# Attention scores for the row maxima, computed as pairs of heads on row groups of the matmul array

## The reference, cut to what matters

```python
    # B, T, D, H = 2, 1024, 128, 16 ; HD = 8
    q, k, v = (proj(Wq, bq), proj(Wk, bk), proj(Wv, bv))
    q = q * cos + rotate_half(q) * sin
    k = k * cos + rotate_half(k) * sin
    attn = jnp.einsum('bhqd,bhkd->bhqk', q, k) * scale
    attn = jax.nn.softmax(attn, axis=-1)
    out = jnp.einsum('bhqk,bhkd->bhqd', attn, v)
```

## Time and profile before

| | before |
|---|---|
| median of 3 runs | 1059.84 us (1059.75 to 1062.03) |
| profiled execution, its own time | 1058.78 us |
| span of its trace, first to last instruction | 1057.0 us |
| mean granted PE clock | 0.906 |
| PE busy | 862.0 us (82%) |
| DVE busy | 862.0 us (82%) |
| ACT busy | 572.5 us (54%) |
| attention passes, on PE | from 88.57 us |

### The profile page before, as it was taken

The page is one execution under the profiler, slowest core; times in us unless marked ns, Lnnn a source line. Parts: engine busy times, 40 slices in busy tenths (PEclk is TensorE's granted clock), DMA queues, the critical chain, the costliest instruction groups (busy, mean ns, idle before and its releaser), DMA issues. The chain is left out here.

```text
span 1057.0 us, 12554 instructions
## 1 busy us (share of the span) xinstructions
PE 862.0 (82%) x3703; PEld 392.3 (37%) x3703; DVE 862.0 (82%) x795; ACT 572.5 (54%) x897; POOL 238.8 (23%) x131
## 2 busy tenths in 40 slices
PE   5589999989999949985464457777777579999998
PEld 2212222222222212224342222222222266888886
DVE  6698888878888748828956899999999873888886
ACT  2304777767777737882131642332333165888885
POOL 3700000000000000100110156776777620123110
PEclk9857999999999979998677788998999867999999
DMA  7440020110101030003000233444444002122111
GB/s 174 128 132 1 11 56 24 54 58 12 56 11 57 14 99 11 11 20 85 0 1 0 89 119 118 160 158 140 158 159 158 21 1 83 60 97 83 60 60 41
DMA packets 37977, 73.51 MB, mean 70 GB/s; under 512 B 7299, under 2 KB 21627, under 8 KB 36891
## 3 DMA queue, kind: packets, MB, share of 16 engines
q1 hardware_dynamic: 37922, 72.82, 21.7%
HBM read 62.50 MB, written 8.85 MB: 68 GB/s over the span
## 5 line engine op out<-in xcount | busy, mean ns | idle before, releaser
L970 DVE TENSOR_REDUCE nmax<-ps 128x1 f32<-128x1024 f32 x256 | 301.0, 1218 | 57.3 <-PE ps L1291 57.3
L738 ACT ACTIVATE prob<-ps 128x512 f32<-128x512 f32 x512 | 265.7, 605 | 137.1 <-PE ps L1310 136.8
L1291 PE MATMUL ps<-ks,qs 96*128 96x512 bf16 x512 | 206.3, 416 | 29.7 <-DVE nmax L970 18.1
L1310 PE MATMUL ps<-qs,ks 96*128 96x512 bf16 x512 | 194.7, 389 | 7.0 <-ACT prob L738 3.3
L670 POOL TENSOR_TENSOR hc<-hst,cbr 128x1024 f32<-128x1024 f32 x64 | 153.4, 2398 | 93.1 <-DVE hst L1107 93.1
L1489 PE MATMUL ps<-hc,ident 128*128 128x512 f32 x256 | 134.4, 650 | 41.7 <-POOL hc L670 38.8
L862 ACT ACTIVATE ps<-dt,a_neg 128x1024 f32<-128x1024 f32 x64 | 71.5, 1118 | 145.9 <-DVE hst L1107 145.9
L1107 DVE TENSOR_TENSOR_SCAN hst<-ps,dbx 128x1024 f32<-128x1024 f32 x64 | 145.6, 2276 | 0.0
L1327 PE MATMUL ps<-prob,vq 128*16 128x512 f32 x1024 | 133.6, 598 | 0.8 <-ACT prob L738 0.7
L1174 DVE TENSOR_TENSOR act_l<-act_t,act_h 128x1024 fp32r<-128x1024 f32 x64 | 92.1, 1449 | 35.5 <-ACT act_h L903 35.5
L1310 PEld LDWEIGHTS ps<-qs,ks 96*128 96x128 bf16 x512 | 49.6, 98 | 164.6 <-ACT prob L738 117.5
(11 more groups left out here) (176 smaller groups left out, 969.7 us busy)
## 6 DMA issues: line engine op xcount, KB each, us to landing
cbr<-s_dram SPq DMA_DIRECT2D x64, 512.0 KB, 3.6
gate<-c_dram SPq DMA_DIRECT2D x8, 1024.0 KB, 6.7
qs<-q_dram SPq DMA_DIRECT2D x18, 288.0 KB
ks<-k_dram SPq DMA_DIRECT2D x54, 96.0 KB
o_dram<-o_sb SPq DMA_DIRECT2D x16, 256.0 KB, 2.1
wf<-in_L_ffn_w SPq DMA_DIRECT2D x8, 256.0 KB, 2.8
wfq<-in_L_ffn_w SPq DMA_DIRECT2D x8, 256.0 KB, 3.1
q_dram<-parts SPq DMA_DIRECT2D x16, 96.0 KB, 2.1
```

Source lines behind the costliest of these rows:

```text
L738: nc.scalar.activation(prob[:, n % 8], ps[:, 4 + (first + n) % 3], ACT.Exp, scale=ATT_SCALE).then_inc(s_exp, 1)
L970: nc.vector.tensor_reduce(nmax[:, half, n:n + 1], ps[:, 2 * (t % 2):2 * (t % 2) + 2, :], AX.XY, ALU.max, negate=True).then_inc(s_max, 1)
L1291: mm = nc.tensor.matmul(ps[:, 2 * (t % 2) + kk], qs[p][:, half, h, q * P:(q + 1) * P], ks[p][:, kk, h, :], start=True, stop=True)
L1310: nc.tensor.matmul(ps[:, 4 + (first + n) % 3], ks[p][:, kt // 4, j, kt % 4 * P:(kt % 4 + 1) * P], qs[p][:, half, j, :], start=True, stop=T ...
```

## The change

- The untransposed score tiles, whose only use is the maxima, are made by `score_pair` in place of `score_half`. They use two bf16 parts of q and k in place of three: 4 products of 8 numbers, 32 rows for each head. The four heads lie in four row groups of new tiles `qm[p]` and `km[p]`; one pair is two heads, 128 queries by 512 keys each.
- DVE's reduce gives one maximum for each head (two outputs for 1024 inputs); one `tensor_tensor` with `min` per half pass joins the two halves of the keys.
- The new tiles are filled by `load_heads`: 2 x 4 x 3 = 24 DMAs for each set, issued on the SP queue immediately before `load`, at the start for three sets and then in each of passes 0 to 5.
- In a step both pairs come in one place, after the fourth matmul of line 1310 and before `products`.
- `rden` becomes a view of the tile `sq`.

```diff
+        qm, km = ([sb(f"{w}{n}", [P, 2, BANK], BF16) for n in range(SETS)] for w in ("qm", "km"))
...
+        nmax_k = sb("nmax_k", [P, 2, 2, QUAD, 4])
...
-        rden = sb("rden", [P, BATCH, SEQ])
+        rden = sq[:].rearrange("p (b t) c -> p b (t c)", b=BATCH)
...
+            def load_heads(it, p):
+
+                for f in range(2):
+                    for h in range(QUAD):
+                        q, k = (t[bass.ds(it, 1), f].rearrange("o n (d h) t -> (o n d) h t", h=QUAD)[0:2 * HD, h]
+                                for t in (q_dram, k_dram))
+                        sp.dma_start(km[p][32 * h:32 * h + 32, f], k.unsqueeze(0).to_broadcast([2, 2 * HD, BANK])).then_inc(s_qm[p], 16)
+                        for a in range(2):
+                            sp.dma_start(qm[p][32 * h + 16 * a:32 * h + 16 * a + 16, f],
+                                         q[HD * a:HD * a + HD].unsqueeze(0).to_broadcast([2, HD, BANK])).then_inc(s_qm[p], 16)
...
             for p in range(SETS):
+                load_heads(p, p)
                 load(p, p)
...
                 if again is not None:
                     sp.wait_ge(s_pv, STEPS * (it + 1))
+                    load_heads(again, p)
                     load(again, p)
...
-                        dve.wait_ge(s_score, 32 * it + t + 1)
-                        nc.vector.tensor_reduce(nmax[:, half, n:n + 1], ps[:, 2 * (t % 2):2 * (t % 2) + 2, :],
-                                                AX.XY, ALU.max, negate=True).then_inc(s_max, 1)
...
+                        u = 16 * half + n
+                        qt, kk, pair = n // 4, n % 4 // 2, n % 2
+                        dve.wait_ge(s_score, 32 * it + u + 1)
+                        nc.vector.tensor_reduce(nmax_k[:, half, kk, 2 * pair:2 * pair + 2, qt], ps[:, 2 * pair:2 * pair + 2, :],
+                                                AX.X, ALU.max, negate=True).then_inc(s_max, 1)
+                    w = 3 * (2 * it + half)
                     dve.wait_ge(s_max, 32 * it + 16 * half + 16)
+                    nc.vector.tensor_tensor(nmax[:, half], nmax_k[:, half, 0].rearrange("p h q -> p (h q)"),
+                                            nmax_k[:, half, 1].rearrange("p h q -> p (h q)"), ALU.min).then_inc(s_mstep, 1)
...
+            def score_pair(it, p, u):
+
+                half, qt, kk, pair = u // 16, u % 16 // 4, u % 4 // 2, u % 2
+                if not (isinstance(it, int) and it == 0 and u < 2):
+                    pe.wait_ge(s_max, 32 * it + u - 1)
+                for n in range(2):
+                    rows = slice(32 * (2 * pair + n), 32 * (2 * pair + n + 1))
+                    mm = nc.tensor.matmul(ps[:, 2 * pair + n], qm[p][rows, half, qt * P:(qt + 1) * P],
+                                          km[p][rows, kk, :], start=True, stop=True)
+                mm.then_inc(s_score, 1)
...
-                        for t, kk in todo[len(todo) * j // 4:len(todo) * (j + 1) // 4]:
-                            score_half(it + 1, (p + 1) % SETS, t, kk)
+                        if more and j == QUAD - 1:
+                            for u in range(MAX_TILES):
+                                score_pair(it + 1, (p + 1) % SETS, MAX_TILES * s + u)
                         if s >= 1 and j == (QUAD - 1 if more else QUAD - 2):
                             products(it, p, s - 1)
```

More of the change, by code:

```diff
@@ L227, in build_kernel @@
         s_qk = [sem(f"s_qk{n}") for n in range(SETS)]
+        s_qm = [sem(f"s_qm{n}") for n in range(SETS)]
         s_score = sem("s_score")
@@ L439, in build_kernel @@
         LOADS = 16 * (2 * (PARTS + 1) + 1)
+        HEAD_LOADS = 16 * 2 * 3 * QUAD
         @block.sync
@@ L967, in maxima @@
                     for n in range(16):
-                        t = 16 * half + n
-                        dve.wait_ge(s_score, 32 * it + t + 1)
-                        nc.vector.tensor_reduce(nmax[:, half, n:n + 1], ps[:, 2 * (t % 2):2 * (t % 2) + 2, :],
-                                                AX.XY, ALU.max, negate=True).then_inc(s_max, 1)
-                    w = 2 * (2 * it + half)
+                        u = 16 * half + n
[4 more added lines that the diff above has]
+                    w = 3 * (2 * it + half)
                     dve.wait_ge(s_max, 32 * it + 16 * half + 16)
+                    nc.vector.tensor_tensor(nmax[:, half], nmax_k[:, half, 0].rearrange("p h q -> p (h q)"),
+                                            nmax_k[:, half, 1].rearrange("p h q -> p (h q)"), ALU.min).then_inc(s_mstep, 1)
+                    dve.wait_ge(s_mstep, w + 1)
                     nc.vector.tensor_copy(nmax_p[:, 0:16], nmax[:, half]).then_inc(s_mstep, 1)
-                    dve.wait_ge(s_mstep, w + 1)
+                    dve.wait_ge(s_mstep, w + 2)
                     nc.vector.tensor_tensor(nmax_p[:, 16:32], nmax[:, half], nmax_p[:, 0:16], ALU.subtract).then_inc(s_mstep, 1)
-                    dve.wait_ge(s_mstep, w + 2)
+                    dve.wait_ge(s_mstep, w + 3)
                     dve.wait_ge(s_nrow[half], 64 * it)
@@ L1008, in _ @@
             dve.wait_ge(s_qk[SETS - 1], LOADS * (PASSES // SETS + 1))
+            dve.wait_ge(s_qm[SETS - 1], HEAD_LOADS * (PASSES // SETS + 1))
             quant(0, wf[:], wfq[:], (s_wf, 16 * 5), scaled=lambda: norm_dve_var(1, 0), before_last=lambda: norm_dve_scale(1, 0))
@@ L1284, in _, with one_pass @@
                 mm.then_inc(s_v_ps, 1)
[L1286 to L1296, removed]
+            def score_pair(it, p, u):
[7 more added lines that the diff above has]
+                mm.then_inc(s_score, 1)
+            def one_pass(it, p, first, loads, more, between={}):
+                pe.wait_ge(s_qk[p], LOADS * loads)
                 for s in range(STEPS):
@@ L1303, in one_pass @@
                     if more and s == 0:
-                        pe.wait_ge(s_qk[(p + 1) % SETS], LOADS * loads)
-                    todo = [(MAX_TILES * s + n // 2, n % 2) for n in range(2 * MAX_TILES)] if more else []
+                        pe.wait_ge(s_qm[(p + 1) % SETS], HEAD_LOADS * (loads + (p + 1) // SETS))
                     for j in range(QUAD):
@@ L1329, in products @@
                 mm.then_inc(s_pv, 1)
-            pe.wait_ge(s_qk[0], LOADS)
+            pe.wait_ge(s_qm[0], HEAD_LOADS)
             pe.wait_ge(s_v, 4)
-            for t in range(32):
-                score_half(0, 0, t, 0)
-                score_half(0, 0, t, 1)
+            for u in range(32):
+                score_pair(0, 0, u)
             with pe.Fori(0, PASSES // SETS) as r:
                 for p in range(SETS):
-                    one_pass(SETS * r + p, p, 4 * STEPS * p, True, r + 1 + (p + 1) // SETS)
-            one_pass(PASSES - 2, 0, 0, True, PASSES // SETS + 1)
+                    one_pass(SETS * r + p, p, 4 * STEPS * p, r + 1, True)
+            one_pass(PASSES - 2, 0, 0, PASSES // SETS + 1, True)
             def project_out(b):
@@ L1412, in turn_first_x @@
                 turn_x(1, 1)
-            one_pass(PASSES - 1, 1, 4 * STEPS, False, between={1: lambda: project_out(0), 8: turn_weights, 12: turn_first_x})
+            one_pass(PASSES - 1, 1, 4 * STEPS, PASSES // SETS + 1, False, between={1: lambda: project_out(0), 8: turn_weights, 12: turn_first_x})
             pe.wait_ge(s_wft, 3)
```

## The result

The changed kernel takes 1164.14 us (median of 4 runs, 1159.64 to 1166.09) against 1060.28 us before: the ratio is 1.097, 95% interval 1.0936 to 1.1005. The forecast was 1168 us. The profiled execution took 1166.09 us, its span is 1164.3 us.

The account below looks back on a forecast made before the run. The passes were taken to run at PE's pace, with SP's added DMAs delaying it: 44.8 + 8.5 + 18.3 + 35.7 + 1 = 108.3 us on 1058.8 gives 1167.1, forecast 1168 us, range 1137 to 1199.

Parts of the forecast that it names:

- Start: Before pass 0: 72 added DMA issues at 0.70 us delay the first maxima; pass 0 starts 35.7 us later.
- Passes 1, 2, 4, 5: PE stalls 9.4 us at step 8 for second-half maxima, plus 1.8 us of lowered clock: 44.8 us in all.
- Pass 3: Same step 8 stall, less because PE already starts 2.7 us late: 6.7 + 1.8 = 8.5 us.
- pass 6: `den` comes 18.3 us later behind SP's issues, delaying DVE's maxima of pass 7 and PE's second step: 18.3 us.
- Steps: 72 steps outside the waits take 2.83 us, row-group savings lost to waiting for ACT: about 1 us in all.
- P: Time of a step's pair matmuls on PE: 0.22 us if all overlap, 0.87 if none; about 0.34 taken.
- Rival 1: SP's added issues are cheap, 0.436 us each, so stalls total about 57 us: 1117 us; chance 0.15.
- rival 2: Row groups on PE don't overlap: step 3.36 us, 40 us more, 1206 us; chance 0.14.
- Rival 3: The added DMAs' transfers are slow, carried by few engines, 4.7 us more at nine places: about 1210 us; chance 0.06.
- Rival 4: Kernel gets faster: step falls to DVE's 2.35 us and SP's work hides, ending near 1055 us; chance 0.05.
- The range: Total time from 1137 us at 0.60 us an SP issue to 1199 at 0.90, the latter adding about 139 us.

Follow-up runs that it names:

- the run with two queues: Changed kernel with heads issued earlier, in mid pass, start reordered, pairs before the fourth matmul, and ACT issuing all `km` DMAs before pass 0: 1059.95 us, ratio 0.9998.
- the best version: Changed kernel with earlier mid-pass heads, reordered start, pairs before the fourth matmul, rows over more DMA engines, ACT issuing sets 1 and 2's heads at start: 1051.91 us.

## Why the prediction was right

The time and the cause were right, and the terms can be laid against the account above. That the sum came out within 1 us of the trace (108.3 forecast, 107.3 measured) is luck in part: single terms are off by 1 to 3 us both ways, and 4.5 us of what was measured, in pass 0 and from pass 7 on, had no term of its own.

- **Start, 35.7 us forecast, 32.6 measured.** The last stores of parts ended 46.5 us later, not 50.4: an issue with its gap took 0.65 us, not 0.70. The price came from line 503, whose shape is like theirs but whose issue is longer: 0.684 us against 0.624. SP then waited 1.6 us before the maxima, for which the forecast had nothing, and PE started 1.3 us after the fourth of them was issued, not 2.1. What followed had no term: the granted clock was 0.51 from 121 to 133 us, and pass 0 took 1.4 us more than before.
- **Passes 1, 2, 4, 5, 44.8 us forecast, 43.1 measured.** Step 8 resumed 31.1 us after the pass began; the forecast had 31.5. Two errors in it nearly cancel: the 24 issues took 18.9 us, not 18.3, and PE started 1.3 us after the fourth issue's end and not 2.1. The 2.1 us were read from stores of 256 KB, and those of the maxima have 2 KB. That the clock falls after a stall of 8.65 us, as it did after 13.70, was needed for this term and held (0.50 from 201 to 207 us).
- **Pass 3, 8.5 us forecast, 7.3 measured; pass 6, 18.3 forecast, 19.8 measured.** That the same queue delay would come out in full through `den` was read from a stall that PE already had. PE's wait grew by 17.8 us. The other 2 us are the clock behind the stall, at half for some 7 us in place of 4 (0.50 from 485 to 494 us, with PE at work from 487.15; before, 0.50 from 383 to 387).
- **Steps, 2.83 us forecast, 2.71 and 2.83 in turn.** Both values were in the forecast, as bounds of P: 2.71 when all four run together, 2.83 when DVE holds the second pair. I took one as the rule where they alternate. In 72 steps that is 4 us. The wait of the fourth matmul for the first exponential was forecast 1.08 us after the first and stands there. It takes back 0.43 of the 0.65 us that the four matmuls save.
- **Rival 1** (cheap issues) falls by the 0.62 us, **rival 2** (row groups don't overlap) by the 0.32 us from the pairs to the products. The Trainium skill (TensorE: Matmul & The Clock Gate, Measured speedup vs the span model) gave an estimated 0.28 us for the four. In the trace the 0.32 us hold the change to the products too, some 0.1 us, which leaves 0.22: the four ran wholly together, and faster than that estimate. The mean step, 2.77 us, equals the one that the estimate gave, but by chance: it is the mean of 2.71 and DVE's 2.83.
- **Rival 3** (slow transfers) was wrong for the changed kernel and right as a mechanism. In the run with two queues an average of 1.8 engines carried them, and a set took some 17.8 us from the first issue (40.92) to the first pair (58.72), though its issues took only 11.3 us; with another dimension outermost it took 5 us less. The Trainium skill (DMA: Bandwidth & Descriptors, Why a DMA increments its semaphore by 16 and not by 1) gives these DMAs two engines, and the trace agrees with 1.8.
- **Rival 4** (faster): the part of it that lies on PE is real. With the issues out of the way and the pairs in front of the fourth matmul, the best version is 7 us below the kernel before. The kernel before with SP's and ACT's work at the start in the new order was not run; in its trace PE never waits for a DMA of the maxima, so little of the 7 us should be due to the order alone, but this is argued. Three things remain in the way. DVE's buffer of two makes every other step long. The start is later: 53.97 us for the first pair in the best version, against 50.76 for the first such matmul before. And the clock falls more often: passes 4 and 5 of the best version take 44.6 us at a granted clock of 0.96, where its pass 1 takes 43.0 at 1.00; the kernel before has 1.00 in both.
- **The range.** By the forecast's own terms 0.90 us an issue gives 143 us and not 139, so the upper end should have been 1203. Nothing hangs on it.

What was only argued: that a deeper buffer for DVE would bring the step down to 2.39 us. PSUM has no bank left for it (four for the pairs, three for the rotation, one for the products), and it wasn't tried.

## What to carry to other kernels

A DMA costs its issuing queue time, one after another, and the bytes say little about how much: here 0.35 us for 256 KB (a plain store), 0.61 for 2 KB, 0.62 for 16 KB and 0.81 for 288 KB. Before adding DMAs, list what stands behind them on that queue with the moment at which each is wanted; a slack of 8.9 us took 18.9 us of issues here, and lost 11 us a pass. Do the same for the place that they are moved to. And when work on an engine is shortened or gathered in one place, look for the wait that it covered: here four matmuls saved 0.65 us a step, and the wait for an exponential took 0.43 of it back until the order was changed.

## What the runs showed of the hardware that was not expected

- Matmuls on four row groups of 32 rows ran fully together, 0.32 us from their start to the next arrangement for four of 512 columns, although each pair has a wait of its own before it.
- The three changes of arrangement in a step (score to row groups, row groups to products, products to score) each cost about 0.1 us; none was dearer for the row groups.
- Changing which dimension of a small DMA is outermost moved its issue by -0.03 and +0.06 us and changed the number of DMA engines at work: in the same 6 us of the start the share of the two queues rose from 11.2% to 23.2%, from 1.8 engines in the mean to 3.7.
- In some versions the granted clock fell at the turn of a pass where the kernel before kept it: in the best one it is 0.80 from 318.6 to 327.0 us, the first steps of pass 5. Why it falls there is open; in the version with the early start and the pairs before the fourth matmul it is 1.00 in passes 4 and 5.
